# Fourth attention layer of a four-layer kernel: keys placed from SBUF instead of through DRAM, and the order of the value products

## What is computed

```
qt = conv1x1(x, w_q, b_q).reshape(BS * N_HEADS, H * W, -1)
xp = avg_pool_3x3_s2_same(x)
kt = conv1x1(xp, w_k, b_k).reshape(BS * N_HEADS, H * W // 4, -1)
vt = conv1x1(xp, w_v, b_v).reshape(BS * N_HEADS, H * W // 4, -1)
attn = softmax(einsum('bnd,bmd->bnm', qt, kt) / TEMP)
out = einsum('bnm,bmd->bnd', attn, vt).reshape(BS, H, W, -1)
return conv1x1(out, w_o, b_o) + residual
```

## Time and profile before

| what | us |
|---|---|
| median of 3 runs | 135.91 |
| lowest and highest run | 134.63, 136.24 |
| span of the profiled execution | 133.3 |
| median less this span (what lies around it) | 2.6 |
| TensorE busy | 121.4 (91%) |
| VectorE busy | 84.4 (63%) |
| ScalarE busy | 76.7 (58%) |
| GpSimd busy | 73.0 (55%) |

### The profile page before, as it was taken

One profiled execution on the slowest core, in us unless ns is written; L12 is line 12 of the kernel. 1 busy time (PEld: TensorE's weight loads), 2 busy tenths in 40 slices (PEclk: granted clock), 3 DMA queues, 4 the chain that ended last, 5 costly groups with the idle time before them and its releaser, 6 DMA issues.

```text
span 133.3 us, 3594 instructions
## 1 busy us (share of the span) xinstructions
PE 121.4 (91%) x1382; PEld 88.7 (67%) x1382; DVE 84.4 (63%) x196; ACT 76.7 (58%) x228; POOL 73.0 (55%) x120
## 2 busy tenths in 40 slices
PE   6686999999999999999899985999859999999990
PEld 4474999987875867765678861423333675988990
DVE  5867877563323736688788332699699999940081
ACT  0436387699885385676987540434334657597320
POOL 8942639998961132310089888305067666799300
PEclk9999999999999999999999998699995999999999
DMA  4960000000000000000000042434554710000046
GB/s 63 319 216 0 0 5 2 0 2 2 0 5 0 5 0 0 5 0 0 0 0 5 22 136 79 120 91 126 82 82 139 73 11 5 5 0 5 5 128 187
DMA packets 19104, 6.41 MB, mean 48 GB/s; under 512 B 9360, under 2 KB 18960, under 8 KB 19088
## 3 DMA queue, kind: packets, MB, share of 16 engines
q1 hardware_dynamic: 17456, 4.93, 15.7%
q10 hardware_dynamic: 1632, 1.27, 3.7%
HBM read 4.61 MB, written 1.57 MB: 46 GB/s over the span
## 4 chain that ended last, share of the span: by engine, by line
PE 76%; DVE 11%; DMA 4%; issue 3%; POOL 2%; ACT 1%; ACTq 0%; DVEq 0%
PE bank L752 11%; PE bank L697 9%; PE bank L795 8%; PE bank L774 8%; PE bank L783 5%; PE bank L716 5%; PE bank L736 5%; DMA x_all<-in_x_dram 4%; PE bank L749 3%; PE bank L688 3%; PE bank L812 3%; PE bank L681 2%; PE bank L726 2%; PE bank L763 2%; DVE prob L590 2%
## 5 line engine op out<-in xcount | busy, mean ns | idle before, releaser
L417 ACT ACTIVATE prob<-bank,negmax 128x256 f32<-128x256 f32 (+1 forms) x48 | 19.3, 409 | 13.0 <-DVE negmax L550 10.1
L356 POOL TENSOR_TENSOR prob<-prob,inv 128x512 f32<-128x512 f32 x16 | 16.3, 1042 | 16.2 <-DVE inv L600 16.2
L468 ACT ACTIVATE prob<-prob 128x512 f32<-128x512 f32 x16 | 10.1, 631 | 20.0 <-DVE prob L590 20.0
L774 PE MATMUL bank<-kdiag,qT 128*32 128x512 f32 x128 | 17.9, 683 | 2.1 <-issue 2.1
L752 PE MATMUL bank<-probT,v 128*128 128x256 f32 x64 | 16.9, 387 | 0.4 <-issue 0.4
L697 PE MATMUL bank<-packed,xT 128*128 128x128 f32 (+1 forms) x96 | 15.6, 286 | 0.2 <-ACT prob L417 0.2
L578 DVE SCALAR_TENSOR_TENSOR xT<-bank,packed,xT 128x256 f32<-128x256 f32 x16 | 7.7, 484 | 12.6 <-PE bank L752 7.8
L697 PEld LDWEIGHTS bank<-packed,xT 128*128 128x128 f32 x96 | 13.1, 191 | 1.9 <-issue 1.2
L795 PEld LDWEIGHTS bank<-probT,vdiag 128*32 128x32 f32 x512 | 11.5, 112 | 3.0 <-issue 3.0
L752 PEld LDWEIGHTS bank<-probT,v 128*128 128x128 f32 x64 | 11.2, 190 | 3.2 <-issue 2.1
L588 DVE TENSOR_REDUCE negmax<-bank 128x8 f32<-128x512 f32 x16 | 10.6, 663 | 3.7 <-PE bank L774 3.5
(11 more groups left out here) (102 smaller groups left out, 242.6 us busy)
## 6 DMA issues: line engine op xcount, KB each, us to landing
kdiag<-k_rows SPq DMA_DIRECT2D x32, 64.0 KB, 2.5
out_dram<-x_all SPq DMA_DIRECT2D x8, 128.0 KB, 1.9
x_all<-in_x_dram SPq DMA_DIRECT2D x2, 256.0 KB, 4.8
x_all<-in_x_dram ACTq DMA_DIRECT2D x2, 256.0 KB, 5.8
vdiag<-v_rows SPq DMA_DIRECT2D x8, 64.0 KB, 3.2
packed<-in_pack_dram ACTq DMA_DIRECT2D x1, 321.0 KB, 6.2
k_rows<-kT SPq DMA_DIRECT2D x4, 64.0 KB, 2.2
v_rows<-vt SPq DMA_DIRECT2D x4, 64.0 KB, 2.0
```

What stands on the lines that cost most here:

```text
L356: nc.gpsimd.tensor_tensor(p, p, inv[g][:, t, :].unsqueeze(2).broadcast_to([128, HEADS, KEYS]), ALU.mult)\
L417: last = nc.scalar.activation(prob[g][:, t, 0:keys], psum("scores", layer, g)[:, keys * t:keys * t + keys], ACT.Exp, bias=negmax[g][:, t, ...
L468: nc.scalar.activation(prob[g][:, t, :], prob[g][:, t, :], ACT.Exp).then_inc(s_exp3, 1)
L774: last = mm(ps[STRIP * s:STRIP * s + STRIP, :].rearrange("p (c m k) -> p c k m", c=HEADS, m=HKEY), qT[g][:, 0, HTOK * j:HTOK * j + HTOK], ...
```

## The change

The columns of the key weights and the key bias are put in another order on the host: channel 16k+e goes to place 8e+k ("chunk innermost"). `kT[i]` then already has, in its 8 partitions 8e to 8e+7, the rows that belong into partition 16c+e of a diagonal block. So `place_keys` copies `kT[i]` itself, SBUF to SBUF, 8 times; the DRAM tensor, `write_keys` and the wait for its landing are gone, and SyncE waits for `s_key_rows` in their place. In `apply3` the loops over strips and pairs are exchanged, so that consecutive products write different partitions.

```diff
+    def by_channel(a):
+        return a.reshape(*a.shape[:-1], HEADS, DH).swapaxes(-1, -2).reshape(a.shape)
...
-        {"w3q": i["L3_conv_w_q"], "w3k": i["L3_conv_w_k"], "w3v": i["L3_conv_w_v"], "w3o": i["L3_conv_w_o"],
-         "bk3": column(i["L3_conv_b_k"]), "bo3": column(i["L3_conv_b_o"]), "bv3": everywhere(i["L3_conv_b_v"])},
+        {"w3q": i["L3_conv_w_q"], "w3k": by_channel(i["L3_conv_w_k"]), "w3v": i["L3_conv_w_v"], "w3o": i["L3_conv_w_o"],
+         "bk3": column(by_channel(i["L3_conv_b_k"])), "bo3": column(i["L3_conv_b_o"]), "bv3": everywhere(i["L3_conv_b_v"])},
...
-        k_dram = [nc.dram_tensor(f"k_rows{i}", (128, PAIR * PTOK), f32, kind="Internal").ap() for i in range(IMAGES // PAIR)]
...
-            def write_keys(i):
-                sp.wait_ge(s_key_rows, i + 1)
-                sp.dma_start(k_dram[i], kT[i][:, :]).then_inc(s_keys_out[i], 16)
-
             def place_keys(i):
...
-                sp.wait_ge(s_keys_out[i], 16)
-                rows = k_dram[i].rearrange("(c e) n -> e c n", e=DH)
+                sp.wait_ge(s_key_rows, i + 1)
                 for c in range(HEADS):
-                    sp.dma_start(kdiag[i % KEY_BUFFERS][DH * c:DH * c + DH, c, :, :], rows).then_inc(s_keys[i], 16)
+                    sp.dma_start(kdiag[i % KEY_BUFFERS][DH * c:DH * c + DH, c, :, :], kT[i][:, :]).then_inc(s_keys[i], 16)
...
-            write_keys(0)
             place_keys(0)
-            write_keys(1)
             place_keys(1)
-            write_keys(2)
             write_values(0)
             write_values(1)
             place_keys(2)
             place_values(0)
-            write_keys(3)
             write_values(2)
             place_values(1)
             place_keys(3)
...
-                    for p in range(PAIRS):
-                        for s in range(STRIPS):
-                            at, j = HTOK * (STRIPS * t + s), STRIPS * t + s
+                    for s in range(STRIPS):
+                        at, j = HTOK * (STRIPS * t + s), STRIPS * t + s
+                        for p in range(PAIRS):
                             last = mm(ps[STRIP * p:STRIP * p + STRIP, at:at + HTOK],
```

More of the change, by code:

```diff
@@ L210, in build @@
         s_key_rows = sem("key_channels_ready")
-        s_keys_out, s_vals_out = ([sem(f"{n}_in_dram{i}") for i in range(IMAGES // PAIR)] for n in ("keys", "values"))
+        s_vals_out = [sem(f"values_in_dram{i}") for i in range(IMAGES // PAIR)]
         s_keys, s_vals = ([sem(f"{n}_placed{i}") for i in range(IMAGES // PAIR)] for n in ("keys", "values"))
```

## The result

| | before | after |
|---|---|---|
| median of 20 runs each, us | 135.5 (134.17 to 136.35) | 134.19 (132.17 to 136.48) |
| time after over time before | | 0.9896 [0.9856, 0.9935] |
| profiled execution, span | 133.3 | 133.9 (135.68 with what lies around) |

The change gains 1.0%, some 1.4 us (0.9 to 2.0), where 3.8 had been forecast; 2% is not reached. The ratio and its interval leave out the slow executions, the medians take in all: those of before lie at 134.2 to 134.6 (9) and 135.4 to 136.4 (11), those of after at 132.2 to 132.3 (2), 133.5 to 134.9 (13) and 135.4 to 136.5 (5).

A forecast was written before the change was run, and what follows sets the result against it. It took the late first keys, then VectorE's chain with TensorE close behind, to bound the kernel. Span 133.3 − 2.5 (keys, clock) − 1.7 (products) + 0.4 (clock) = 129.5, with 2.6 around it 132.1 us; range 130.4 to 134.2.

The forecast's parts named there:

- I take 431: First pair's key copies from SBUF: 431 ns each to issue, the median of the present copies from DRAM.
- the 2.15: TensorE's wait for the first keys before the fourth layer's first scores, 2.15 us, expected to go.
- The bound from the value placement, 667: Far end for a key copy's issue: 667 ns, the median of placing values; keys would land at about 81.0.
- the one with 0.55 to 0.7 us a copy: Rival, a new wait for the first keys: half or all of the keys' gain goes; 133 to 134.3 us, chance 0.07.
- the products' 1.7: From the last turning to the last products, faster value products were to save 1.7 us.
- the forecast 0.6: An image's 64 value product records in the new order: 0.6 us, against 1.30 to 1.44 before.
- 3.47 to 1.8: TensorE's stretch at the end, from the last turning to the last products, was to take 1.8 us instead of 3.47.
- 1.44 us kept: Rival, same rate of the products by the skill's rule: only the keys gain; 133.4 us, chance 0.13.
- Charged were 0.4 us: TensorE's clock falling to half between 108 and 119 through new idle time: 0.4 us, between 0 and 1.7.
- Credited were 0.3: VectorE's 0.3 us wait at its second maximum, laid to TensorE's low clock after the idle time, was to go.
- the first of the rivals: Clock low at the end: last products and projections at half clock, costing 1.7 instead of 0.4; 133.4 us, chance 0.15.
- Each of these is 2 us or more ahead of its use: Keys of the later pairs arrive 2 us or more early; the fourth pair's come some 5 us earlier than now.

The follow-up runs named there:

- experiment 3: The changed kernel with 20 small products added on TensorE ahead of its wait for the first keys; ratio to before 0.9807, median 133.31 us.
- experiment 4: The kernel before with five sets of eight 64 KB copies, of differing sources and destinations, added at its start; 135.92 us in one run.
- experiment 1: The changed kernel with the product loops as before, so only the keys go straight from SBUF; ratio to before 0.9881, median 133.81 us.
- experiment 6: The changed kernel with four of each pair's eight key copies left out, and so half of the scores' chunks; ratio to before 0.9813, median 132.39 us.
- experiment 7: The changed kernel with two of the first pair's eight key copies issued by ScalarE, six by SyncE; ratio to before 0.983, median 132.71 us.
- experiment 11: The changed kernel with three of the first pair's key copies issued by ScalarE and 20 small products added on TensorE; ratio to before 0.9796, 131.99 us.
- experiment 9: The changed kernel with two of the first pair's key copies issued by ScalarE and 20 small products added on TensorE; ratio to before 0.9785, 132.14 us.
- experiment 10: The changed kernel with 6 small products added on TensorE ahead of its wait for the first keys; ratio to before 0.9889, median 133.72 us.
- experiment 2: The kernel before with only the value products' loops exchanged, keys still through DRAM; ratio to before 0.9891, median 134.21 us.
- experiment 5: The changed kernel with the keys written to DRAM again and read back in rows of 4 KB; ratio to before 0.9922, median 135.18 us.
- the twenty: 20 small products (40 instructions) added on TensorE ahead of its wait for the first keys; on the changed kernel the ratio to before is 0.9807.
- experiment 8: The kernel before with only the value products' loops exchanged, plus 20 small products added on TensorE; ratio to before 0.9861, median 132.78 us.

## Why the prediction was wrong

Two steps failed: the price of a copy, taken as 0.43 us and measured as 0.60, and a term that was put at nothing, TensorE's stand within the faster products, which in the profile took back all that they gain at the end (1.65 us by experiment 3). The 134.19 lies just inside the range of 130.4 to 134.2 that was given, by luck: neither gain came as it was summed.

**The copies: the first step that failed.** "I take 431, since only the source changes and the pieces and the destination do not." The source was what mattered. A copy takes 598 ns in the changed kernel and 598 against 431 by itself (experiment 4). The eight took some 5.1 us where 3.65 were summed, 1.4 more; of the 2.15 there remained 0.8 (0.64 in experiment 1, and 0.5 in the mean of four profiles against four). The prediction's own sum comes out with the right price: 73.42 + 5.1 + 2.06 = 80.6 for the first scores, and 73.39 + 7.29 = 80.68 was found. The bound from the value placement, 667, had the right order of size; of the rivals the one with 0.55 to 0.7 us a copy was true of the keys, and it had 0.07. Its time, 133 to 134.3, holds the measured one, but it kept the products' 1.7, which the profile of after doesn't show. That what the first keys gain reaches the last inversion one to one was right (experiments 6 and 7).

**Products: the rate right, their worth not; the second step that failed.** 0.69 on the chain and 0.76 in the timeline answer to the forecast 0.6. "3.47 to 1.8": without a stand it is 1.97 (experiments 3, 7 and 11), 1.50 us less. With one it is 3.62. The prediction had nothing of this: at 20 ns a record TensorE never stood in before or in experiments 1 and 4, at 11 to 12 it did in 6 of 10 profiles, and in after the stand took back the whole gain. The Trainium skill (TensorE: Matmul & The Clock Gate, Part 3: Packing small matmuls, The mechanism) lets weight loads overlap products in flight only where the row group differs. The prediction read that as 1.44 us kept, since these weights use all rows; the traces do not agree with that reading, with 0.76 for the 64.

**What the stand is.** Its place in the program is shown (experiments 9 and 10). Its operands are there, since the records before it read the same tiles. What it waits for can be read in the DMA view of after, from 117 to 128 us in 40 slices of 0.275 us:

```profile
DMA  0000020000000000000000020000000000000020
...
q8 instruction: 3, 0.05, 1.6%
```

The only packets in these 11 us are three of 16 KB, of the kind "instruction". The first two pass in slices 6 and 24, at 118.4 to 118.65 and at 123.3 to 123.6. TensorE resumes at 120.75 (a stand of 0.29 in image 5) and at 125.77: each time 2.1 to 2.5 us behind a packet. The time is like that from issue to landing of the key copies, 2.6 us. In the six profiles with stands (after and experiments 2, 5, 6, 9 and 10) all twelve stands, two in each, end 2.1 to 3.0 us behind such a packet. The same view of experiment 7, from 113 to 124:

```profile
DMA  0000000000000000000300000000000002000000
...
q8 instruction: 2, 0.03, 1.4%
```

Here the packet passes at 118.2 to 118.5, and the record where after stood comes at 121.23 + 0.33 = 121.56: it is 3.1 us or more ahead, in after 0.7 to 1.0. The three profiles with the twenty and no stand (experiments 3, 8 and 11) agree: a packet passes 2.6 to 3.3 us ahead of the 63rd record of image 6, the place where experiment 9 stood with 1.7 to 1.9. **What fits all ten is that TensorE waits for the next 16 KB of its instructions, and only where they are fetched less than some 2 to 3 us ahead.** That was read from the traces, not tested by a run that moves a packet alone, and that these packets are TensorE's is itself concluded from the agreement. What sets when a packet goes out, and so how often unprofiled runs have the stand, stays open. The ratios bear on the latter: with the twenty they are lower in all three pairs (0.9807 for 0.9896, 0.9861 for 0.9891, 0.9785 for 0.983), by 0.4 to 1.2 us, and the intervals of no pair are apart.

**The clock.** Charged were 0.4 us for a fall that didn't come in after: the window 105:119 shows 1.00, with TensorE idle for 18% of it ((14 − 11.53) / 14), about the fifth foreseen. Credited were 0.3 for the clock at the first scores; without its two falls VectorE's chain is 0.61 shorter, but experiment 2 has that too, and so has experiment 4 with the old keys and the old products (35.96). Before doesn't always have them, then. A late fall, the first of the rivals, came in experiment 11: the clock was at 0.50 from 118 to 120, and a group of 64 products took 1.06 us. It cost nothing at the end there, since the last turning ended 4.39 us behind the last inversion as elsewhere.

**Later pairs.** "Each of these is 2 us or more ahead of its use" was wrong for the fourth: its copies go out 2.3 us earlier than in before (97.10 − 75.11 against 97.71 − 73.39), not 5, and take 5.09 us, and TensorE waits 0.50 us for them at 104.31. VectorE binds there and took it up; the last inversion shows nothing of it.

**What lies around the span.** 2.6 us was the median less the profiled span. The profiled executions of after and of the experiments have 1.8 to 1.9, so 0.8 of the 2.6 was spread between runs. This error had the other sign.

**Sum.** Forecast −2.5 −1.7 +0.4 = −3.8; found −1.41 (keys 0.80, clock 0.61) and +0.16 from there to the end: −1.25 between the two profiles. Of this only the keys' part, 0.3 to 0.8 over all profiles, is shown to come of the change.

## What to carry to other kernels

A transfer's price to issue belongs to its two ends as much as to its shape: a row with the same pieces but another source is not the nearest row, and eight copies in one queue turn 0.17 us into 1.4. Where a detour through DRAM is removed, count what the queue then has to issue, and split it over two queues. A gain that comes from issuing small instructions faster should be looked for at the end of the chain itself, since a stand within them can take it all back, as it did in the profile of after. And a gain of some tenths of a microsecond needs more than one profile of the old kernel: the same way of the keys took 7.72 to 8.09 us here.

## What the runs showed that was not expected

- The same 64 KB take 0.60 us to issue from SBUF to SBUF and 0.42 to 0.43 from DRAM to SBUF, in 128 pieces or in 16.
- TensorE stands still for 0.3 to 1.5 us inside unbroken groups of small products, at places that move one record for each record that is added ahead, and goes on 2.1 to 3.0 us behind a packet of 16 KB of the kind "instruction" (12 stands in 6 profiles).
- Products with 128 active rows whose outputs go round the four strips of PSUM partitions ran at 0.69 to 0.76 us for 64 records, 11 to 12 ns each, against 20 to 22 when they stayed in one.
